# The last head of a linear attention: decayed values from eight exponentials of their own, keys turned ahead of the outputs, probabilities by halves between state steps

## The reference

```python
def step(S, inp):
    q_t, k_t, v_t, b_t = inp
    b = b_t[..., None, None]
    S = (1.0 - b) * S + b * (v_t[..., :, None] * k_t[..., None, :])
    o_t = jnp.einsum('bhvk,bhk->bhv', S, q_t)
    return (S, o_t)
_, os = lax.scan(step, S0, (qs, ks_, vs, bs))
o = os.transpose(1, 0, 2, 3).reshape(Bs, Ls, H * DV)
o = o * gate
return o @ Wo
```

## Time and profile before

| | |
|---|---|
| median of 3 runs | 1059.94 us (1059.01 to 1061.52) |
| profiled execution | 1060.79 us |
| its span, first to last instruction | 1059.0 us |
| mean granted clock of TensorE | 0.985 |
| TensorE / VectorE / ScalarE / GpSimd busy | 95% / 73% / 64% / 51% |
| linear attention's last outputs end, late part begins | about 765 us |

### The profile page before, as it was taken

How to read it: one execution, slowest core, us unless ns; L and a number is a source line. 1 busy time by engine, 2 the same in 40 slices (tenths; PEclk the granted TensorE clock), 3 DMA queues, 4 the chain that set the end, 5 groups by cost and what they waited for, 6 DMA issues and landing times.

```text
span 1059.0 us, 19066 instructions
## 1 busy us (share of the span) xinstructions
PE 1008.1 (95%) x6781; PEld 795.1 (75%) x6781; DVE 769.0 (73%) x1567; ACT 679.6 (64%) x1244; POOL 541.1 (51%) x454
## 2 busy tenths in 40 slices
PE   7999999999999998699999999999899999999997
PEld 4333333467888896598988989899799788888997
DVE  5889999646766845899998999899766465344843
ACT  4588888766554347888887888888645353333454
POOL 3351310114069551889888898898315001447543
PEclk9999999999999999899999999999999999999999
DMA  4443443223224201543244233421311124555100
GB/s 98 88 78 58 77 68 58 61 88 94 80 88 134 39 1 34 197 145 106 96 154 142 106 105 135 150 105 66 125 32 41 46 61 104 155 149 167 61 21 21
DMA packets 83626, 96.21 MB, mean 91 GB/s; under 512 B 29912, under 2 KB 68524, under 8 KB 81484
## 3 DMA queue, kind: packets, MB, share of 16 engines
q1 hardware_dynamic: 82800, 94.05, 31.4%
q10 hardware_dynamic: 732, 0.95, 0.3%
HBM read 82.29 MB, written 1.41 MB: 79 GB/s over the span
## 4 chain that ended last, share of the span: by engine, by line
PE 54%; DVE 11%; POOL 4%; ACT 4%; issue 3%; DVEq 2%; DMA 1%; POOLq 0%; ACTq 0%
PE late_bank L65 7%; PE late_bank L67 7%; PE late_bank L66 7%; PE lin_pair L65 3%; PE lin_pair L67 3%; PE lin_pair L66 3%; PE lin_pair L1863 3%; DVE lin_conv_k L2250 2%; PE gold_bank L65 2%; PE gold_bank L67 2%; PE gold_bank L66 2%; PE lin_pair L1960 2%; DVE gold_part L1476 2%; PE lin_pair L1949 2%; DVE lin_conv_q L2250 2%
## 5 line engine op out<-in xcount | busy, mean ns | idle before, releaser
L744 ACT ACTIVATE attn_probs<-attn_rows_k 128x512 f32<-128x512 f32 x256 | 138.9, 595 | 24.4 <-PE attn_rows_k L590 21.2
L590 PE MATMUL attn_rows_k<-attn_q_stack,attn_k_stack 50*128 50x512 f32 x256 | 94.0, 446 | 0.0
L3063 DVE TENSOR_TENSOR late_mids<-late_mids,late_bank 128x512 f32<-128x512 f32 (+1 forms) x50 | 34.3, 687 | 77.8 <-PE late_bank L67 74.8
L855 DVE TENSOR_REDUCE attn_row_max<-s_sum 128x1 f32<-128x1024 f32 x62 | 75.6, 1220 | 10.9 <-PE attn_rows_q L574 5.0
L603 PE MATMUL attn_ctx<-attn_probs,attn_v 128*32 128x256 f32 x1024 | 81.5, 391 | 1.5
L855 DVE TENSOR_REDUCE attn_row_max<-attn_rows_q 128x1 f32<-128x1024 f32 x62 | 75.9, 1224 | 8.9 <-PE attn_rows_q L574 5.4
L65 PE MATMUL late_bank<-net_x_part_low,late_w_T 128*128 128x512 f32 (+1 forms) x192 | 77.9, 405 | 0.0
L66 PE MATMUL late_bank<-net_x_part_low,late_w_T 128*128 128x512 f32 (+1 forms) x192 | 76.1, 396 | 0.0
L67 PE MATMUL late_bank<-net_x_part_low,late_w_T 128*128 128x512 f32 (+1 forms) x192 | 76.1, 396 | 0.0
L3163 POOL TENSOR_TENSOR late_mids<-late_mids,late_raw_w_T_last 128x512 f32<-128x512 f32 x22 | 29.5, 1363 | 90.2 <-DMA late_raw_w_T_last<-top_weights 90.2
L1611 POOL TENSOR_TENSOR gold_mids<-gold_mids,s_later 128x512 f32<-128x512 f32 x32 | 51.9, 1660 | 45.5 <-DMA s_later<-gold_weights 45.5
(11 more groups left out here) (478 smaller groups left out, 3551.1 us busy)
## 6 DMA issues: line engine op xcount, KB each, us to landing
s_raw_w_o<-query_norms SPq DMA_DIRECT2D x16, 1024.0 KB, 4.8
lin_mix<-decay_sums SPq DMA_DIRECT2D x16, 512.0 KB, 6.0
lin_q_dec<-decay_sums SPq DMA_DIRECT2D x16, 512.0 KB, 7.2
s_later<-gold_weights SPq DMA_DIRECT2D x16, 256.0 KB, 3.6
attn_k_stack<-s_part SPq DMA_DIRECT2D x30, 128.0 KB, 3.5
s_raw_ring<-in_L_ffn_Wg SPq DMA_DIRECT2D x12, 256.0 KB, 2.8
s_raw_ring<-in_L_ffn_Wu SPq DMA_DIRECT2D x12, 256.0 KB, 3.1
attn_k_stack<-s_part SPq DMA_DIRECT2D x33, 64.0 KB, 2.3
```

What stands on the lines that cost most here:

```text
L590: pe.matmul(out, k_stack[rows, h % SLOTS, t * P:(t + 1) * P], q_stack[rows, h % SLOTS, :], start=True, stop=True).then_inc(scored_k, 1)
L744: act.activation(probs[:, (2 * k + odd) % PB, side * HALF:(side + 1) * HALF], ring_bank(("exped", 4 * k + n + 1)), ACT.Exp).then_inc(exped, 1)
L855: dve.tensor_reduce(row_max[h % 2][:, tile:tile + 1], ps_tile[tile_bank(n)][:, :], axis=AX, op=ALU.max)\
```

## The change

- `add_end` (GpSimd) adds `mix_bias` to the last column of the masked logarithms of head 15, 128x8, and `exp_end` (ScalarE) takes their exponential, ahead of the key norms. `last_decay_v` multiplies the values by that, for seven tiles instead of eight, and so waits no longer for `exp_mix`.
- TensorE turns the keys of head 15 ahead of the outputs of head 14. ScalarE copies its keys ahead of its queries.
- The key rows are made for seven tiles instead of eight.
- `last_key_values`, `last_score` and `last_outputs` take the place of the three functions for head 15. They announce their first halves, and the outputs wait tile by tile: for the first or second half of the probabilities, and for the state step that they need. Their first waits are for the decayed queries and the gate of head 14.
- `last_steps` (VectorE) does the copy and step 1, half of the probabilities, step 2, the other half, step 3, and then steps 4 to 6. Before, it did all states and then all probabilities.

```diff
--- before.py
+++ after.py
@@ -1698,6 +1698,7 @@
         self.z, self.soft, self.log_b, self.log_rest = (
             self.probs[:, n, :].rearrange("p (c h) -> p c h", c=NT) for n in (4, 5, 6, 7))
         self.mix_bias = sb("mix_bias", [P, NT, LH])
+        self.end_decay = sb("end_decay", [P, NT, 1])
         self.e_last = sb("e_last", [P, NT, LH])
         self.pair = [ps(f"pair{n}", [P, T]) for n in range(4)]
         self.tiled = [p[:, :].rearrange("p (c d) -> p c d", c=NT) for p in self.pair]
@@ -1730,6 +1731,8 @@
         self.masked, self.mix_exped, self.q_dec_done = sem("masked"), sem("mix_exped"), sem("q_dec_done")
         self.scored, self.kv_done, self.probs_done, self.states_done, self.o_done, self.gated = (
             sem(n) for n in ("scored", "kv_done", "probs_done", "states_done", "o_done", "gated"))
+        self.end_added, self.end_exped, self.kv_half, self.scored_half, self.probs_half, self.state_steps = (
+            sem(n) for n in ("end_added", "end_exped", "kv_half", "scored_half", "probs_half", "state_steps"))
 
 
 
@@ -1950,10 +1953,7 @@
             i.then_inc(self.scored, 1)
 
         def key_values(h):
-            if h + 1 < LH:
-                pe.wait_ge(self.g_acted, h + 1)
-            else:
-                pe.wait_ge(self.states_done, h)
+            pe.wait_ge(self.g_acted, h + 1)
             pe.wait_ge(self.k_rows_done, h + 1)
             pe.wait_ge(self.v_dec_done, h + 1)
             for c in range(NT - 1):
@@ -1964,15 +1964,53 @@
             pe.wait_ge(self.probs_done, h + 1)
             pe.wait_ge(self.states_done, h + 1)
             pe.wait_ge(self.q_dec_done, h + 1)
-            if h + 1 < LH:
-                pe.wait_ge(self.k_normed, h + 2)
-            else:
-                pe.wait_ge(self.gated, h)
+            pe.wait_ge(self.k_normed, h + 2)
             for c in range(NT):
                 cols = slice(c * P, (c + 1) * P)
                 i = pe.matmul(pair[2][:, cols], self.v_rows[h // 2 % 2][:, c, h % 2, :], self.probs[:, c, :], start=True,
                               stop=(c == 0))
                 if c:
+                    i = pe.matmul(pair[2][:, cols], self.state[:, c, :], self.q_dec[h % 2][:, cols], start=False, stop=True)
+            i.then_inc(self.o_done, 1)
+
+        def last_key_values():
+            h = LH - 1
+            pe.wait_ge(self.states_done, h)
+            pe.wait_ge(self.k_rows_done, h + 1)
+            pe.wait_ge(self.v_dec_done, h + 1)
+            for c in range(NT - 1):
+                i = pe.matmul(tiled[0][:, c, :], self.k_rows[:, c, :], self.v_dec[:, c, :], start=True, stop=True)
+                if c == NT // 2 - 1:
+                    i.then_inc(self.kv_half, 1)
+            i.then_inc(self.kv_done, 1)
+
+        def last_score():
+            pe.wait_ge(self.q_T_done, LH)
+            pe.wait_ge(self.k_T_done, LH)
+            for c in range(NT):
+                cols = slice(c * P, (c + 1) * P)
+                i = pe.matmul(pair[1][:, cols], self.k_T[:, cols], self.q_T[:, cols], start=True, stop=True)
+                if c == NT // 2 - 1:
+                    i.then_inc(self.scored_half, 1)
+            i.then_inc(self.scored, 1)
+
+        def last_outputs():
+            h = LH - 1
+            pe.wait_ge(self.q_dec_done, h + 1)
+            pe.wait_ge(self.gated, h)
+            for c in range(NT):
+                cols = slice(c * P, (c + 1) * P)
+                if c == 0:
+                    pe.wait_ge(self.probs_half, 1)
+                if c == NT // 2:
+                    pe.wait_ge(self.probs_done, h + 1)
+                i = pe.matmul(pair[2][:, cols], self.v_rows[h // 2 % 2][:, c, h % 2, :], self.probs[:, c, :], start=True,
+                              stop=(c == 0))
+                if c:
+                    if c < NT - 1:
+                        pe.wait_ge(self.state_steps, c)
+                    else:
+                        pe.wait_ge(self.states_done, h + 1)
                     i = pe.matmul(pair[2][:, cols], self.state[:, c, :], self.q_dec[h % 2][:, cols], start=False, stop=True)
             i.then_inc(self.o_done, 1)
 
@@ -2000,11 +2038,11 @@
                 project_v(n)
             else:
                 project_gate(LH - 1)
+                turn_k(LH - 1)
             outputs(n - 2)
-        turn_k(LH - 1)
-        key_values(LH - 1)
-        score(LH - 1)
-        outputs(LH - 1)
+        last_key_values()
+        last_score()
+        last_outputs()
 
     def high(self, act, m, src, done):
         act.activation(self.parts[m][0][:, :, :], src[:, :, :], ACT.Copy).then_inc(done, 1)
@@ -2079,6 +2117,10 @@
             for c in range(NT):
                 i = act.activation(mix[:, c, :], mix[:, c, :], ACT.Exp, bias=self.mix_bias[:, c, h:h + 1])
             i.then_inc(self.mix_exped, 1)
+
+        def exp_end():
+            act.wait_ge(self.end_added, 1)
+            act.activation(self.end_decay[:, :, :], self.end_decay[:, :, :], ACT.Exp).then_inc(self.end_exped, 1)
 
         def tap(h, m, pair, projected, rowed, done):
             act.wait_ge(projected, h + 1)
@@ -2172,10 +2214,11 @@
         k_transposed(LH - 2)
         silu_gate(LH - 2)
         high_gate(LH - 1)
+        exp_end()
         norm_k(LH - 1)
         exp_mix(LH - 1)
+        k_transposed(LH - 1)
         q_transposed(LH - 1)
-        k_transposed(LH - 1)
         silu_gate(LH - 1)
 
     def dve_first(self, dve):
@@ -2233,6 +2276,38 @@
                 i = dve.scalar_tensor_tensor(self.state[:, c + 1, :], self.state[:, c, :], self.e_last[:, c, h:h + 1],
                                              self.tiled[0][:, c, :], ALU.mult, ALU.add)
             i.then_inc(self.states_done, 1)
+
+        def last_steps():
+            h = LH - 1
+
+            def probs_half(half):
+                tiles = slice(half * NT // 2, (half + 1) * NT // 2)
+                return dve.tensor_tensor(self.probs[:, tiles, :], self.tiled[1][:, tiles, :], self.mix[h % 3][:, tiles, :], ALU.mult)
+
+            def step(c):
+                return dve.scalar_tensor_tensor(self.state[:, c + 1, :], self.state[:, c, :], self.e_last[:, c, h:h + 1],
+                                                self.tiled[0][:, c, :], ALU.mult, ALU.add)
+
+            dve.wait_ge(self.o_done, h)
+            dve.wait_ge(self.kv_half, 1)
+            dve.tensor_copy(self.state[:, 1, :], self.tiled[0][:, 0, :]).then_inc(self.state_steps, 1)
+            dve.drain()
+            step(1).then_inc(self.state_steps, 1)
+            dve.wait_ge(self.mix_exped, LH)
+            dve.wait_ge(self.scored_half, 1)
+            probs_half(0).then_inc(self.probs_half, 1)
+            dve.drain()
+            step(2).then_inc(self.state_steps, 1)
+            dve.wait_ge(self.scored, LH)
+            probs_half(1).then_inc(self.probs_done, 1)
+            dve.drain()
+            step(3).then_inc(self.state_steps, 1)
+            dve.wait_ge(self.kv_done, LH)
+            for c in range(4, NT - 2):
+                dve.drain()
+                step(c).then_inc(self.state_steps, 1)
+            dve.drain()
+            step(NT - 2).then_inc(self.states_done, 1)
 
         def convolve(h, m, pair, tapped, done):
             if m == 0 and h >= 1:
@@ -2280,10 +2355,11 @@
         def last_rows_k():
             dve.wait_ge(self.k_normed, LH)
             dve.wait_ge(self.kv_done, LH - 1)
-            rows = [self.norm_row[:, j, :].rearrange("p (o d) -> p o d", o=1).to_broadcast((P, NT, HD)) for j in range(2)]
-            dve.tensor_tensor(self.k_rows[:, :, :], self.normed_k[:, :, :], rows[0], ALU.mult)
+            rows = [self.norm_row[:, j, :].rearrange("p (o d) -> p o d", o=1).to_broadcast((P, NT - 1, HD)) for j in range(2)]
+            read = self.k_rows[:, 0:NT - 1, :]
+            dve.tensor_tensor(read, self.normed_k[:, 0:NT - 1, :], rows[0], ALU.mult)
             dve.drain()
-            dve.tensor_tensor(self.k_rows[:, :, :], self.k_rows[:, :, :], rows[1], ALU.add).then_inc(self.k_rows_done, 1)
+            dve.tensor_tensor(read, read, rows[1], ALU.add).then_inc(self.k_rows_done, 1)
 
         def last_centre_q():
             dve.wait_ge(self.norms_loaded, 16 * LH)
@@ -2329,8 +2405,7 @@
             if live(n):
                 variances(n, 0, 3, self.q_rowed, self.stats_turned, self.q_var)
                 variances(n, 1, 2, self.k_rowed, self.k_rstd, self.k_var)
-        states(LH - 1)
-        probs(LH - 1)
+        last_steps()
         between(dve)
         gate(LH - 1)
 
@@ -2393,6 +2468,21 @@
             last = self.mix[h % 3][:, :, P - 1:P].to_broadcast((P, NT, HD))
             pool.tensor_tensor(self.v_dec[:, :, :], self.v_rows[h // 2 % 2][:, :, h % 2, :], last, ALU.mult)\
                 .then_inc(self.v_dec_done, 1)
+
+        def add_end():
+            h = LH - 1
+            pool.wait_ge(self.bias_ready, 1)
+            pool.wait_ge(self.masked, LH)
```

(13 more changed lines are left out.)

## The result

The changed kernel takes 1056.60 us (median of 20 runs) where the kernel before, run beside it, takes 1061.69. The ratio is 0.9951, with a 95% interval of 0.9933 to 0.9968: 5.2 us faster, between 3.4 and 7.1. Two later comparisons of the same two kernels gave 0.9971 (0.9952 to 0.9991) and 0.9972 (0.9944 to 0.9999).

The account below looks back on a forecast made before the run. TensorE, busy 95% of 1059.0 us, was taken as the bound, with holes at the last linear-attention head. The late part moving from 765.03 to 760.02 wins 5.0 us, from median 1059.94 to 1054.9; range 1053.2 to 1057.2.

Parts of the forecast that it names:

- The place of the hole: Last linear-attention head: added logarithms and exponentials cost 0; decayed values run 746.73 to 748.39; key-values follow without a hole.
- The blocking: VectorE's first key row operation waits for GpSimd's decayed values: cost between 0 and 1.02 us, taken as 1.02.
- The first rival: No blocking: GpSimd and VectorE don't hinder each other at the key rows; 6.0 us won, 1053.9 us; chance 0.13.
- Queries, scores, decayed queries: Last head: queries copied by 754.17, scores 754.25 to 756.1 behind a 0.95 us hole, outputs from 756.65 behind decayed queries.
- Outputs to the late part: Last head's outputs take 3.37 us from 756.65; late part starts at 760.02, its first split ready at 759.6.
- The third head: Output projection: the third head begins at 762.9, when VectorE's split is ready; just in time, an error costs tenths.
- The clock: TensorE at 2.4 GHz throughout, its hole shrunk from 2.27 to 0.95 us; rival of half clock in outputs, chance 0.09.
- The halves and the extra waits: Last head: eight new output waits cost 0 to 0.8 us, taken as 0; VectorE's halves and steps 1 us off path.
- The weights' landing: Remaining output weights land at 762.3, are ready at 765.2 and wanted at 765.8: hidden, 0.6 us to spare.
- The sum: Late part from 765.03 to 760.02: 5.0 us won, forecast 1054.9 us; chance 0.62.

Follow-up runs that it names:

- e1: Changed kernel with GpSimd's decayed values made for one tile instead of seven (work left out); ratio to the kernel before 0.9966 (0.9942 to 0.9989).
- e7: Kernel of e6 with decayed values made by ScalarE and the large exponentials by halves around the queries' copy; ratio to the kernel before 0.9945 (0.9914 to 0.9976).
- e8: Changed kernel with seven more waits, all fulfilled, in VectorE's queue ahead of the last head's steps; one execution, time not compared, late part at 15.77 us.
- e6: Changed kernel with VectorE's last gate moved behind the low parts of heads 2 and 3; ratio to the kernel before 0.9938 (0.9915 to 0.9961).
- e2: Changed kernel with VectorE in the old order, all states and then both halves of the probabilities; ratio to the kernel before 0.9987 (0.9946 to 1.0029).
- e4: Changed kernel without the addition and eight exponentials, decayed values from the large exponentials again; ratio to the kernel before 0.9977 (0.9951 to 1.0002).
- e5: Kernel before with only the eight exponentials and the seven tiles of decayed values added; ratio to the kernel before 0.9982 (0.9954 to 1.0011).
- e0: Changed kernel again, no edit, for a profile at TensorE's usual clock; ratio to the kernel before 0.9971 (0.9952 to 0.9991).
- e9: Changed kernel unchanged, timed beside the kernel of e7; median 1057.98 us, ratio to the kernel before 0.9972 (0.9944 to 0.9999).

## Why the prediction was right

**The place of the hole.** Right. The added logarithms took 0.21 us and the exponential 0.21 with its table load, both hidden; the decayed values moved from behind the exponentials to 2.36 behind the common start, and lasted 1.69 (predicted 1.66).

**The blocking.** Right, and it was the term that decided between 6.0 and 5.0. Predicted 1.02 us, measured 2.10 - 1.09 = 1.01, and e1 shows the same 1.00 at the late part. The exclusive lock of the Trainium skill (page SBUF — State Buffer, section "SBUF: two separate sides") agrees with this: VectorE's operation, with two SBUF inputs, ended at 748.13, 0.94 us behind GpSimd's end at 747.19, a little less than the 1.09 that it takes alone. The first rival had spoken against it.

**Queries, scores, decayed queries.** Right: a hole of 0.97 (predicted 0.95), then outputs at 12.38 from the common start (predicted 756.65 - 744.33 = 12.32). The decayed queries were what they waited for.

**Outputs to the late part.** Mis-sized. I had 3.37 from the row of before; it took 3.60. VectorE lost 0.44 us between two steps, which the rows of before that I used did not show, and so the first split was ready at 759.07 and TensorE went on at 759.12. The slack of 0.4 that I had given this split was eaten by it. Where the stretch is 0.22 (e7, e8) the outputs take 3.38.

**The third head.** "Just in time, and an error here costs tenths": it cost 0.30, at 762.33, where TensorE waited for VectorE's split. e6 shows that moving the last gate behind this split is enough to remove it. A shorter idle stretch alone is not: in e8 it is 0.22 shorter, and from the late part to the router's weights it is still 13.47.

**The clock.** Right for the profiled executions: it is 1.00 all through. The key-values took 1.73 us instead of the 3.34 of before and ended 0.97 ahead of the queries; at the old length they would have ended 0.6 behind them.

**The halves and the extra waits.** The waits between output products cost nothing that the trace shows: two records each still take a step of 0.22, and in e7 and e8 the outputs take 3.38 with them and 3.37 without them in the kernel before. The halves are worth 0.8 at the late part and 0.5 in the end (e2). I had only said that VectorE is off the path with them.

**The weights' landing.** Hidden, as predicted: issued behind the queries at about 753.0, landed 7.1 later at 760.1, and ScalarE came to it at 760.23.

**The sum.** 5.0 predicted, 4.72 at the late part, 4.36 behind the ninth head, 5.2 (3.4 to 7.1) in the times. Of the 0.3 missing at the late part, 0.23 are the outputs' term. The repetitions gave 3.1 (1.0 to 5.1) and 3.0 (0.1 to 5.9) in the times. That the first comparison came within 0.2 of the 5.0 is therefore partly luck; what bears the prediction out is the marks, term by term. The forecast of 1054.9 us was 1.7 under the median of 1056.6, because the three runs of before that it started from had a median 1.75 below that of twenty.

## What to carry to other kernels

When work is moved from one engine into another's wait, look at who it now runs beside: GpSimd's operation was wanted by nobody for three microseconds and still took one from VectorE's, and through it from TensorE. Splits and gates that stood ahead of an engine's next stage were covered by the wait that a change removes; reorder them for the new end. And compare edits of a microsecond by marks in the trace counted from a common instruction, since those repeat to hundredths where the times scatter by microseconds.

## What the runs showed that I had not expected

- The length of one hole does not tell whether TensorE's clock falls. It fell behind holes of 2.27 us (before) and 1.88 (e4), and stayed behind 2.44 (before) and 2.32 (e5).
- VectorE has an idle stretch of 0.22 or 0.44 us with no releaser, at one place in its stream of instructions. Seven added waits move it by a step and halve it. The kernel before has two like it, 0.23 and 0.22 us, among the state steps of earlier heads (at 487.79 and 640.11), and none in its last head.
- The same kernel reached the common start at 743.14 and at 746.37 in two profiled executions (e0, e9), over code that the change does not touch. That is 3.2 us of the 4.4 between their spans (1053.6 and 1058.0); the other 1.2 lie behind the router's weights. The cause was not looked for.
